# A decoder layer on one core: attention outputs turned one slot later, statistics taken one slot after the sum, queries projected a slot before keys, six leading self pairs

## The reference, cut to what matters

```python
x = _layernorm(x + attn(x, wq, bq, wk, bk, wv, bv, wo, bo))     # 16 heads of 8, softmax over 128 keys
x = _layernorm(x + xattn(ctx, x, ctx, Wk, Wq, Wv, Wo))          # queries from x, keys and values from ctx
x = _layernorm(x + ffn(x, W1, b1, W2, b2))                      # 128 -> 512 -> 128, gelu, int8-like quantising
```

## Time and profile before

| what | value |
|---|---|
| time, median of 3 runs | 364.69 us (363.92 to 365.56) |
| the profiled execution | 363.44 us, of which the span in the trace is 361.7 us |
| busy in the span | VectorE 90%, TensorE 74%, ScalarE 70%, GpSimd 52% |
| chain that ended last | VectorE 40% (L801 alone 18%), TensorE 20%, issue 17%, GpSimd 10%, ScalarE 5% |
| stages | start and leading self pairs 0 to 68 us, the even part of attention 68 to 264 us, last outputs to 283 us, feed-forward to the end |

### The profile page before, as it was taken

How to read it: one execution, slowest core, us unless ns; L and a number is a source line. 1 busy time by engine, 2 the same in 40 slices (tenths; PEclk the granted TensorE clock), 3 DMA queues, 4 the chain that set the end, 5 groups by cost and what they waited for, 6 DMA issues and landing times.

```text
span 361.7 us, 13218 instructions
## 1 busy us (share of the span) xinstructions
PE 265.9 (74%) x4899; PEld 170.5 (47%) x4899; DVE 325.1 (90%) x720; ACT 252.0 (70%) x502; POOL 187.8 (52%) x382
## 2 busy tenths in 40 slices
PE   3668878898988988889888898888785276201980
PEld 2445545565665655656556565555552131000550
DVE  5657798999999999999999999999989689998994
ACT  2136877787878878788787887778773299803875
POOL 5245778566665665655666656666312003600285
PEclk9999999999999999999999999999998556855796
DMA  1352332323233233232332323322000000000024
GB/s 51 95 160 69 86 91 62 103 71 107 82 91 100 70 107 90 79 103 77 99 96 79 105 70 110 102 86 77 24 4 3 0 0 0 0 0 3 0 89 145
DMA packets 48998, 25.19 MB, mean 70 GB/s; under 512 B 6440, under 2 KB 48808, under 8 KB 48936
## 3 DMA queue, kind: packets, MB, share of 16 engines
q1 hardware_dynamic: 48216, 24.02, 23.1%
q10 hardware_dynamic: 720, 0.33, 0.3%
HBM read 9.39 MB, written 2.10 MB: 32 GB/s over the span
## 4 chain that ended last, share of the span: by engine, by line
DVE 40%; PE 20%; issue 17%; POOL 10%; ACT 5%; SPq 4%; DMA 3%; DVEq 0%; POOLq 0%; ACTq 0%
DVE neg_max L801 18%; DVE h_ext L907 5%; PE ps L1033 5%; DVE h_ext L908 4%; PE ps L1075 4%; PE ps L1059 4%; ACT probs L635 3%; POOL rstd L502 2%; SPq L364 2%; DVE r_sum L811 2%; DMA arena_h<-parts_sk 2%; DVE arena_q L818 1%; POOL o_root L569 1%; PE ps L1083 1%; PE ps L1192 1%
## 5 line engine op out<-in xcount | busy, mean ns | idle before, releaser
L801 DVE TENSOR_REDUCE neg_max<-ps 128x8 f32<-128x1024 f32 x128 | 155.8, 1217 | 11.3 <-PE ps L1033 9.8
L624 ACT ACTIVATE probs<-ps 128x1024 f32<-128x1024 f32 x64 | 65.6, 1025 | 19.3 <-PE ps L1040 18.2
L1033 PE MATMUL ps<-arena_h 31*128 31x128 f16 x1024 | 52.5, 221 | 34.7 <-DVE neg_max L801 23.8
L635 ACT ACTIVATE probs<-ps 128x1024 f32<-128x1024 f32 x64 | 65.7, 1026 | 17.0 <-PE ps L1040 15.5
L1033 PEld LDWEIGHTS ps<-arena_h 31*128 31x128 f16 x1024 | 30.9, 94 | 67.1 <-DVE neg_max L801 42.6
L499 POOL TENSOR_TENSOR var_eps<-mean_var,eps_col 128x1 f32<-128x1 f32 x64 | 12.2, 191 | 81.1 <-DVE mean_var L848 81.1
L1040 PE MATMUL ps<-arena_h 32*128 32x128 f16 x1024 | 51.3, 218 | 0.6 <-ACT probs L624 0.5
L1059 PE MATMUL ps<-probs,arena_q 128*32 128x128 f32 x1024 | 41.2, 279 | 0.9 <-issue 0.9
L1059 PE MATMUL ps<-probs,arena_h 128*32 128x128 f32 x1024 | 41.2, 279 | 0.2 <-ACT probs L624 0.2
L502 POOL TENSOR_TENSOR rstd<-var_eps,minus_half 128x1 f32<-128x1 f32 x64 | 35.2, 550 | 5.2 <-POOL var_eps L499 0.2
L1040 PEld LDWEIGHTS ps<-arena_h 32*128 32x128 f16 x1024 | 29.4, 93 | 1.6 <-issue 0.9
(11 more groups left out here) (155 smaller groups left out, 638.8 us busy)
## 6 DMA issues: line engine op xcount, KB each, us to landing
arena_h<-parts_sq SPq DMA_DIRECT2D x48, 64.0 KB, 1.9
arena_h<-parts_ck SPq DMA_DIRECT2D x48, 64.0 KB, 2.0
arena_h<-parts_cq SPq DMA_DIRECT2D x48, 64.0 KB, 2.0
arena_h<-parts_sk SPq DMA_DIRECT2D x45, 64.0 KB, 2.0
xT_in<-in_xT_dram SPq DMA_DIRECT2D x16, 128.0 KB, 2.3
xN_in<-in_xN_dram SPq DMA_DIRECT2D x16, 128.0 KB, 2.2
cT_in<-in_cT_dram SPq DMA_DIRECT2D x16, 128.0 KB, 2.7
cN_in<-in_cN_dram SPq DMA_DIRECT2D x16, 128.0 KB, 2.3
```

The source lines that it names most:

```text
L624: act.activation(probs[1][:, :], ps_s2, ACT.Exp, scale=SCALE).then_inc(ex, 1)
L635: act.activation(probs[0][:, :], ps_s2, ACT.Exp, scale=SCALE).then_inc(ex, 1)
L801: dve.tensor_reduce(neg_max[b.par][:, HH * half:HH * half + HH], ps_s1.rearrange("p (h k) -> p h k", h=HH), AXX, ALU.max, negate=True).the ...
L1033: ins = pe.matmul(ps_s1[:, at:at + S], q[r:r + MAX_AT, j, :], kk[r:r + MAX_AT, j, :], start=True, stop=True, skip_group_check=True)
```

## The change

- `LEAD_PAIRS` becomes 6. The load of x is issued 8 slots ahead instead of 7.
- The turn of the unnormalised attention (task k-2) moves from behind `product(0)` to behind `product(1)` on TensorE; its reciprocal and normalising on VectorE move from between the two maxima to behind the second, around the residual sum: reciprocal, y of task k-3, normalising.
- The turn of the normalised attention moves from the end of slot k to behind `product(0)` of slot k+1; its copy on ScalarE moves from the end of the slot to behind the maxima row, ahead of the evacuations.
- Statistics and mean and variance move one slot later, between the two maxima, with the new x of task k-5 (before: k-4) between them. In the last slots (from k = 62) they are taken at once as before.
- GpSimd takes the root of task k-4 behind the key and cross-query splits of the slot instead of ahead of them. The turn of the new x on TensorE and its copy are of task k-6 (before k-4).
- For pairs from the seventh on, queries are projected and evacuated one slot ahead of the keys; for the six leading pairs both stay in one slot.
- The weights' scale (VectorE) is taken in slot 3 instead of 2. `y_sb`, `mean_var` and `rstd` have 4 buffers, `stats` 2.

```diff
-LEAD_PAIRS = 5
+LEAD_PAIRS = 6
...
-XT_AT, XN_AT, CT_AT, CN_AT = 7, 3, 8, 6
+XT_AT, XN_AT, CT_AT, CN_AT = 8, 3, 8, 6
+Q_AT = 6
...
-        self.par = pos % 2
+        self.par, self.place = pos % 2, pos % 4
...
+LATE_STATS = TASKS - 2
+def late_stats(k):
+    return task(k - 4) if k <= LATE_STATS else None
+def outputs(k):
+    if k <= LATE_STATS:
+        places = [k - 5]
+    elif k == LATE_STATS + 1:
+        places = [k - 5, k - 4]
+    else:
+        places = [k - 4]
+    return [task(p) for p in places if task(p) is not None]
+def roots(k):
+    if k <= LATE_STATS:
+        return [task(k - 4)] if task(k - 4) is not None else []
+    return [t for t in outputs(k) if t.pos > LATE_STATS - 4]
...
+def k_pair(k):
+    return S_FIRST.get(k + QK_AT)
+def q_pair(k):
+    i = S_FIRST.get(k + Q_AT)
+    if i is not None and i >= LEAD_PAIRS:
+        return i
+    i = S_FIRST.get(k + QK_AT)
+    return i if i is not None and i < LEAD_PAIRS else None
...
-                v = task(k - 4)
-                if v is not None:
-                    pool.wait_ge(ag, v.pos + 1)
-                    pool.tensor_tensor(var_eps[v.par][:, :], mean_var[v.par][:, 1:2], eps_col[:, :], ALU.add).then_inc(ve, 1)
-                    pool.wait_ge(ve, v.pos + 1)
-                    need(pool, xn, v.pos - 1)
-                    pool.tensor_tensor(rstd[v.par][:, :], var_eps[v.par][:, :], minus_half[:, :], ALU.pow).then_inc(rq, 1)
...
+                for v in roots(k):
+                    pool.wait_ge(ag, v.pos + 1)
+                    pool.tensor_tensor(var_eps[v.par][:, :], mean_var[v.place][:, 1:2], eps_col[:, :], ALU.add).then_inc(ve, 1)
+                    pool.wait_ge(ve, v.pos + 1)
+                    need(pool, xn, v.pos - 3)
+                    pool.tensor_tensor(rstd[v.place][:, :], var_eps[v.par][:, :], minus_half[:, :], ALU.pow).then_inc(rq, 1)
...
+                if x is not None:
+                    act.wait_ge(ta, x.pos + 1)
+                    need(act, oo, x.pos)
+                    act.copy(attT[:, :], ps_x[:, 0:S]).then_inc(tae, 1)
...
-                if w is not None:
-                    act.wait_ge(ta, w.pos + 1)
-                    if v is not None and v.kind == "S":
-                        act.wait_ge(tx, v.m + 1)
-                    need(act, oo, w.pos)
-                    act.copy(attT[:, :], ps_x[:, 0:S]).then_inc(tae, 1)
...
-                b, w, x, v = task(k + 2), task(k - 2), task(k - 3), task(k - 4)
+                b, w, x, late = task(k + 2), task(k - 2), task(k - 3), late_stats(k)
...
                 if k == -5:
                     pair_0()
                 maximum(0)
+                if late is not None:
+                    statistics(late)
+                if k > LATE_STATS:
+                    for t in outputs(k):
+                        new_x(t)
+                if k <= LATE_STATS:
+                    for t in outputs(k):
+                        new_x(t)
+                if late is not None:
+                    mean_variance(late)
+                if k == 1:
+                    folded_weights()
+                if k == 3:
+                    weight_scale()
+                    own_step(dve.reciprocal(w_inv[:, :], w_scale[:, :]))
+                maximum(1)
+                if k == 1:
+                    weight_extremes()
                 if w is not None:
...
-                if v is not None:
-                    dve.wait_ge(rq, v.pos + 1)
...
-                    dve.tensor_scalar(dst, src, mean_var[v.par][:, 0:1], rstd[v.par][:, :],
-                                      ALU.subtract, ALU.mult).then_inc(xn, 1)
+                if x is not None:
+                    dve.wait_ge(oo, x.pos + 1)
...
+                    dve.tensor_tensor(dst, own, residual, ALU.add).then_inc(yy, 1)
                 if w is not None:
                     dve.wait_ge(rs, w.pos + 1)
...
-                maximum(1)
...
-                if x is not None:
-                    dve.wait_ge(oo, x.pos + 1)
...
-                    dve.tensor_tensor(dst, own, residual, ALU.add).then_inc(yy, 1)
-                    dve.wait_ge(yy, x.pos + 1)
-                    dve.bn_stats(stats[:, :], y_sb[x.par][:, :]).then_inc(bs, 1)
-                    dve.wait_ge(bs, x.pos + 1)
-                    dve.bn_aggr(mean_var[x.par][:, :], stats[:, :]).then_inc(ag, 1)
+                if k >= LATE_STATS and x is not None:
+                    statistics(x)
+                    mean_variance(x)
                 if k == 4:
                     weight_ints()
...
+                    if q is not None:
...
+                        last = pe.matmul(ps_o[:, 0:PAIR], wq_g[:, :], xT_in[q % LOADS][:, :], start=True, stop=True,
...
+                    if kk is not None:
+                        if q != kk:
+                            pe.wait_ge(eqk, 2 * kk + 1)
+                        pe.matmul(ps_o[:, PAIR:2 * PAIR], wk_g[:, :], xT_in[kk % LOADS][:, :], start=True, stop=True,
...
                 product(0)
+                if x is not None:
+                    pe.wait_ge(an, x.pos + 1)
+                    need(pe, mte, tasks_to(k))
+                    need(pe, tae, x.pos)
+                    need(pe, txe, s_to(k - 7))
+                    pe.transpose(ps_x[:, 0:S], att[:, :, :].rearrange("p h e -> p (h e)"), ident[:, :]).then_inc(ta, 1)
...
                 if nxt is not None:
                     pe.wait_ge(masks, 1)
                     pe.wait_ge(mx, 2 * nxt.pos + 2)
                     need(pe, mte, nxt.pos)
...
+                if k >= LEAD_SLOTS:
+                    projections()
+                scores(1)
+                product(1)
+                if k < LEAD_SLOTS:
+                    projections()
+                if k == 0:
+                    setup_products()
                 if w is not None:
                     pe.wait_ge(ue, w.pos + 1)
                     need(pe, an, w.pos)
                     for blk in range(2):
                         last = pe.transpose(ps_t[:, blk * S:(blk + 1) * S], u_sb[:, blk * S:(blk + 1) * S], ident[:, :])
                     last.then_inc(tu, 1)
-                scores(1)
-                product(1)
                 if x is not None:
                     pe.wait_ge(tae, x.pos + 1)
                     need(pe, yy, x.pos)
...
                     pe.matmul(ps_o[:, 0:D], attT[:, :], (wo_self if x.kind == "S" else wo_cross)[:, :],
                               start=True, stop=True, skip_group_check=True).then_inc(oo, 1)
-                if w is not None:
-                    pe.wait_ge(an, w.pos + 1)
+                if v is not None and v.kind == "S":
+                    pe.wait_ge(xn, v.pos + 1)
...
                     pe.transpose(ps_x[:, 2 * S:3 * S], x1_all[:, v.m, :], ident[:, :]).then_inc(tx, 1)
```

More of the change, by code:

```diff
@@ L195, in decoder_layer @@
         r_sum, att, attT = sb("r_sum", [128, H]), sb("att", [128, H, E]), sb("attT", [128, S])
[L196 to L198 removed]
+        y_sb = [sb(f"y_sb{i}", [128, D]) for i in range(4)]
+        stats = [sb(f"stats{i}", [128, 6]) for i in range(2)]
+        mean_var = [sb(f"mean_var{i}", [128, 2]) for i in range(4)]
         var_eps = [sb(f"var_eps{i}", [128, 1]) for i in range(2)]
[L200 removed]
+        rstd = [sb(f"rstd{i}", [128, 1]) for i in range(4)]
         x2_all = sb("x2_all", [128, B, D])
@@ L811, in slot @@
                     dve.reciprocal(r_sum[:, :], u[:, :, E]).then_inc(rs, 1)
-                if v is not None:
-                    dve.wait_ge(rq, v.pos + 1)
-                    if v.kind == "S":
-                        dst, src = in_groups(x1_all[:, v.m, :]), by_group(y_sb[v.par][:, :])
-                    else:
-                        dst, src = x2_all[:, v.m, :], y_sb[v.par][:, :]
-                    dve.tensor_scalar(dst, src, mean_var[v.par][:, 0:1], rstd[v.par][:, :],
-                                      ALU.subtract, ALU.mult).then_inc(xn, 1)
+                if x is not None:
+                    dve.wait_ge(oo, x.pos + 1)
+                    if x.kind == "S":
+                        dve.wait_ge(xb, x.pair + 1)
+                        dst, own, residual = y_sb[x.place][:, :], ps_o[:, 0:D], x_bias[x.ring][:, x.half, :]
+                    else:
+                        dve.wait_ge(xn, S_POS[x.m] + 1)
+                        dst, own, residual = (by_group(y_sb[x.place][:, :]), by_group(ps_o[:, 0:D]),
+                                              in_groups(x1_all[:, x.m, :]))
+                    dve.tensor_tensor(dst, own, residual, ALU.add).then_inc(yy, 1)
                 if w is not None:
```

96 lines of the change are left out of this document (42 added, 54 removed).

## The result

Before and after were timed side by side: 364.31 us (363.49 to 365.56) before, **370.28 us** (368.77 to 375.65) after, ratio 1.0147 with a 95% interval of [1.0098, 1.0196]. The change makes the kernel slower by 1.5%; forecast were 350.9 us and a range up to 358.5.

A forecast was written before the change was run, and what follows sets the result against it. VectorE, nearly full, was taken to run in a ring with TensorE, 3.78 us a slot. Terms -10.9 - 1.8 - 1.7 + 0.3 + 0.5 - 0.2 = -13.8 took 363.44 to 349.6; plus 1.25, 350.9 us; range 346.5 to 358.5.

The forecast's parts named there:

- GpSimd's root behind the splits: GpSimd: root comes 1.3 us later behind one split, but has a whole slot (3.57) until the new x, so is covered.
- The steady slots: Slots 10 to 61: from 3.78 to 3.57 us each, gaps 0.50, then 0.50 or 0.70; -10.9 us over 52 slots.
- The price of packing: VectorE between the maxima: statistics 0.20, new x 0.17, mean 0.10 to 0.13 us; behind the second: 0.16, 0.20, 0.20.
- this rule: VectorE: an instruction waiting for the one ahead costs its length and 0.03 us, an independent one its length less 0.09.
- The cover of the output projection: TensorE, second half of a slot: output product ends at 1.62, y wants it at 1.73; margin some 0.1 us.
- The slower rival: Chance 0.06: output product ends later than 1.73 us behind the block, so y, normalising and next maximum wait; 369 us.
- The holds rival: Chance 0.05: in every second slot the new x meets a split's second half just begun; 10 us back, 361 us.
- the hold of 0.1 to 0.2 in every second slot: VectorE's new x meets a GpSimd split's first half, held 0.1 to 0.2 us; gap stays near 0.50 to 0.60.
- its 0.03 a slot: Steady slots: 0.03 us added for imperfect meeting, taking the slot from 3.54 to 3.57.
- The rival that TensorE's second half binds: Chance 0.17: turns' waits use up the 0.1 us margin, second gap stays 0.66 in half the slots; about 355 us.
- The leading part: Start-up to slot 9: root waits -1.8, packing -1.7, exchanged pairs +0.3, load ahead of feed-forward weights +0.5 us.
- The last outputs: Slots 62 to 67: the same reductions, -0.2 us; the stage behind 283 us carried over as it is.

The follow-up runs named there:

- e1: The changed kernel with one move: GpSimd takes the roots of a slot behind all its splits; 354.59 us, ratio 0.9614 to the kernel before.
- e16: The same kernel as e1, run again on another chip beside e15; 355.24 us, ratio 0.9721 to the kernel before.
- e2: The changed kernel with statistics and mean taken at once behind y, as before the change, the root staying where the change put it; 371.52 us.
- e15: e1 with two idle GpSimd additions directly ahead of the query and context-key splits, behind the waits for their projections; 363.79 us, ratio 0.9947 to the kernel before.
- e4: The changed kernel with SyncE issuing the maxima row ahead of the slot's first fill; 388.22 us, ratio 1.0575 to the kernel before.
- e12: e1 with the maxima row's transfer issued by ScalarE instead of SyncE; 365.17 us, ratio 0.9992 to the kernel before.
- e14: e1 with TensorE's waits for a coming pair's stacks moved from the scores to the previous slot's output projection; 359.94 us, ratio 0.9880 to the kernel before.

## Why the prediction was wrong

**The step that failed** is "GpSimd's root behind the splits": "The root now has a whole slot (3.57) until the new x asks for it ... so it is covered." That is true of the root: VectorE waits 0.3 us for it in the whole changed kernel, and the 1.8 of the earlier trace rows is gone. But the 1.3 counts only the split ahead of the root and leaves out that the statistics it reads were moved too; the root starts 1.7 later (2.1 into the slot, not 0.4). What I did not ask at all is what stands behind the root's own wait. The mean comes 1.75 into the slot, and bias, context values and the query and context-key splits are queued behind it on an engine that works in order. I followed the result to its reader, and not the waiting instruction to its followers. The price was 19.9 us of waits; e1, which changes this place alone, has 5.6 and takes 354.6.

**The steady slots** were right in size where nothing is late: forecast 3.57, undisturbed 3.56, gaps 0.50, 0.50 and 0.70. Slot 10 to 61 was to shrink by 10.7; e1 shrinks it by 9.9 and e16 by 10.0. The changed kernel lengthens it by 5.3.

**The price of packing** was right in sum: 0.20, 0.24 and 0.14 between the maxima, 0.16, 0.15 and 0.28 behind the second, where 0.20, 0.17 and 0.10 to 0.13 were forecast for the first three. The mean starts 0.09 before the independent new x has ended, and the earlier trace rows had said so; 0.28 + 0.33 + 0.17 = 0.78 us of instructions stand in a gap of 0.50. The difference of e1 and e2, 3.56 against 3.77 a slot, is what moving the statistics is worth, but not a test of this rule: in e2 VectorE idles in its first gap and is full in its second. The rule of the Trainium skill, "VectorE: DVE Perf Modes", section "The DRAIN you can't avoid", read strictly as the prediction did, would have left no room for these overlaps; the measurement decides against that reading. The section itself adds that a next operation that is not held starts earlier, which agrees with these rows.

**The cover of the output projection**, called the thinnest, held: y waits for it 0.3 us in 210. The slower rival built on it did not happen: the kernel is slower, but by another mechanism, which had no chance of its own. The holds rival did not happen either, nor did the hold of 0.1 to 0.2 in every second slot that the forecast itself granted: from 60 to 270 us, 1 of 59 new x of e1 takes over 0.38, where 28 of 55 did before. The sum had nothing for these holds beyond its 0.03 a slot. The rival that TensorE's second half binds (0.17) is not seen: its own late starts are those behind transfers.

**The leading part** did not gain what was forecast, and which of its terms is wrong stays open. I gave -1.8 - 1.7 + 0.3 + 0.5 = -2.7; slot 10 starts 0.1 later than before in the changed kernel. With the load moved ahead of the weights slot 0 is 1.2 longer (5.61 to 6.79) in this profile, TensorE's first wait for a row being 2.9 instead of 1.73. On SyncE's queue it costs what was forecast: the row is issued at 23.24 instead of 22.72. The rest is not the load's, since slot 0 takes 5.98 to 7.12 in the kernels that issue the row at 23.20 to 23.24. The step to mixed pairs gives the rest back: slots 7 and 8 take 5.12 and 4.80, 2.8 over two undisturbed ones. How much of this belongs to the change can't be told from one profile: e1 reaches slot 10 at 69.0 (slot 0 7.12, slots 7 and 8 5.68 and 4.84), the same kernel as e16 at 66.4 (6.17, 3.88 and 3.46, but slot 9 5.10), which is 1.8 earlier than before.

**The last outputs and the feed-forward stage** moved by -0.1, where -0.2 was forecast for slots 62 to 67.

**What a late split meets.** Single slots of e1 still run long. Slot 25 (4.78) shows why:

```profile
118.39 3.10 SPq L406 DMA_DIRECT2D arena_h<-parts_ck  x3
...
122.16 1.83 SPq L406 DMA_DIRECT2D arena_h<-parts_cq  x3
```

```profile
126.58 0.22 PE L1088 MATMUL ps<-arena_h 31*128 31x128 f16 x1 [1.34 <-DMA arena_h<-parts_cq]
```

The splits were in time, but one issue of the first fill took 1.88 instead of 0.60. Such issues are not of the change's making: from 60 to 270 us, 20 of the 259 issues of SyncE take over 0.8 in the kernel before, 20 after the change and 22 in e1, up to 2.1. The kernel before has 0.3 to 1.8 us between the last landing and TensorE's start and hides most of them. A late split takes this slack away.

What stays open: what makes single issues long, slot 44 (4.40) of e16, and what makes the leading part of one kernel differ by 2.6 us between two profiles. Executions of e1 from 352 to 359 us are in keeping with such accidents, which is not shown; the profiled ones of e1 and e16 took 354.59 and 351.86.

## What to carry to other kernels

When a producer is moved later, list every wait on it, and for each what is queued behind the waiting instruction on its engine; then follow those to the queue that they feed. The root's reader had a slot to spare, while the splits behind it had less than 1.2 us: e15 makes the one of the context keys 1.1 later, and TensorE waits 11.7. An engine that is busy half of the time can carry the chain: read its position by when it stands idle and for whom, not by its share.

The transfer waits of TensorE were here the end of three queues worked off in order, VectorE's, GpSimd's and SyncE's. The cure lay in GpSimd's, by moving one block of code, and reordering SyncE's made it worse (e4).

## What the runs showed of the hardware that was not expected

- A fill of three DMAs holds SyncE's queue for 1.83 to 1.85 us when nothing delays it, 0.61 each, and a row 0.57 (kernel after). Anything behind a fill is that much later, though its own data is ready.
- The DMA of one maxima row issued on ScalarE (e12) takes 0.53 in its queue and moves the next exponentials by 0.38.
- Two semaphore waits ahead of TensorE's scores cost 0.20 in every second slot of e1, also where what they wait for had landed already; with them moved (e14) these slots take 3.46 instead of 3.66.
- Some 20 of 259 DMA issues of SyncE from 60 to 270 us (18 to 26 in the runs of this case) take 0.8 to 2.1 us instead of about 0.6. What makes them long no run shows.
- The first half of a split, a 128 x 256 instruction of GpSimd (0.61), that meets the new x on VectorE holds it: in e15 the new x takes 0.63 instead of 0.33, and the gap behind the first maximum grows from 0.50 to 0.90.
